# Three of eight expert products split into fp32r passes, in a one-core kernel of two feed-forward layers

## The reference, cut to what matters

```python
x = x + ffn0(cond0(x))      # cond0: a matrix per sequence of rank 30; ffn0: eight experts
x = x + ffn1(cond1(x))      # cond1: layer norms with gathered rows; ffn1: four ternary products

# ffn0, the layer of the change
gate = xf @ Wg.T + bg
w    = softmax(top_k(gate, 2))
h    = einsum('td,ehd->teh', xf, W1) + b1          # eight experts, 256 hidden each
h    = gelu(h)
o    = einsum('teh,eoh->teo', h, W2) + b2          # the second product of every expert
out  = sum over the two chosen experts of w * o
```

## Time and profile before

| | us |
|---|---|
| median of 3 runs | 429.69 (429.18 to 429.79) |
| the profiled execution | 429.37 |
| its span, first to last instruction | 427.5 |
| TensorE busy | 412.8 (97%) |
| VectorE busy | 313.6 (73%) |
| ScalarE busy | 292.1 (68%) |
| GpSimd busy | 115.8 (27%) |

### The profile page before, as it was taken

The page is one execution under the profiler, slowest core; times in us unless marked ns, Lnnn a source line. Parts: engine busy times, 40 slices in busy tenths (PEclk is TensorE's granted clock), DMA queues, the critical chain, the costliest instruction groups (busy, mean ns, idle before and its releaser), DMA issues.

```text
span 427.5 us, 5760 instructions
## 1 busy us (share of the span) xinstructions
PE 412.8 (97%) x1812; PEld 269.5 (63%) x1812; DVE 313.6 (73%) x656; ACT 292.1 (68%) x518; POOL 115.8 (27%) x122
## 2 busy tenths in 40 slices
PE   7999899999999999999999999999999999898996
PEld 4755455445566765776567655676577657677774
DVE  5889998978987578648775848678873798666653
ACT  5588877967856864868656783886578475757654
POOL 0138102642624700363162000457034031110000
PEclk9989999999999999999999999999999999999999
DMA  7978646554453350434330250347402210000000
GB/s 263 374 305 229 161 120 182 132 166 117 116 130 114 90 149 20 105 80 131 114 111 20 75 147 2 88 80 193 129 0 66 74 57 2 0 0 25 2 25 27
DMA packets 30360, 45.07 MB, mean 105 GB/s; under 512 B 3733, under 2 KB 22650, under 8 KB 29946
## 3 DMA queue, kind: packets, MB, share of 16 engines
q1 hardware_dynamic: 26413, 34.14, 28.6%
q0 software_dynamic: 3584, 10.49, 7.8%
q10 hardware_dynamic: 333, 0.07, 0.1%
HBM read 40.68 MB, written 4.03 MB: 105 GB/s over the span
## 4 chain that ended last, share of the span: by engine, by line
PE 85%; DVE 4%; ACT 4%; DMA 3%; issue 2%; SPq 1%; POOL 1%; ACTq 0%; DVEq 0%
PE bank L656 23%; PE bank L758 21%; PE bank L794 7%; PE bank L704 7%; PE bank L648 6%; PE bank L743 5%; PE bank L672 2%; PE bank L711 2%; PE bank L841 2%; DMA t_split<-tsS 2%; PE bank L783 1%; DMA muT<-cond_512T_in 1%; ACT mG L908 1%; PE bank L563 1%; SPq L418 1%
## 5 line engine op out<-in xcount | busy, mean ns | idle before, releaser
L656 PE MATMUL bank<-mG,W 128*128 128x512 f32 x256 | 119.6, 593 | 0.0
L908 ACT ACTIVATE mG<-bank,keepP 128x512 f32<-128x512 f32 x128 | 85.3, 687 | 28.5 <-PE bank L648 19.0
L1467 POOL TENSOR_TENSOR rstd<-ve,mhalf 128x4 f32<-128x4 f32 x24 | 32.8, 1365 | 203.7 <-DVE ve L1208 203.6
L1193 DVE TENSOR_TENSOR mG<-mG,gwbs 128x1024 f32<-128x1024 f32 x64 | 77.2, 1218 | 2.1 <-DMA gwbs<-gate_w 1.8
L656 PEld LDWEIGHTS bank<-mG,W 128*128 128x128 f32 x256 | 47.5, 189 | 38.9 <-issue 35.3
L648 PE MATMUL bank<-ts,A 96*128 96x512 f32 x128 | 62.1, 525 | 2.3 <-ACT mG L908 1.6
L973 ACT ACTIVATE G<-bank,keepP 128x512 f32<-128x512 f32 x48 | 32.2, 692 | 27.8 <-PE bank L758 27.7
L1448 POOL DMA_INDIRECT gp<-pgb_in,ixall x32 | 36.3, 1133 | 25.7 <-issue 9.2
L758 PE MATMUL bank<-hB_h,h2w_h 128*128 128x512 f32 x96 | 39.7, 414 | 0.0
L758 PE MATMUL bank<-hA_h,h1w_h 128*128 128x512 f32 x96 | 38.7, 403 | 0.0
L1451 POOL DMA_INDIRECT gcm<-ctm,ixcm x32 | 35.5, 1110 | 9.8 <-issue 9.4
(11 more groups left out here) (243 smaller groups left out, 782.2 us busy)
## 6 DMA issues: line engine op xcount, KB each, us to landing
gwbs<-gate_w SPq DMA_DIRECT2D x32, 512.0 KB, 5.5
keep<-xT_in SPq DMA_DIRECT2D x8, 256.0 KB, 5.0
outT<-keep SPq DMA_DIRECT2D x8, 256.0 KB, 2.4
t_split<-tsS SPq DMA_DIRECT2D x7, 192.0 KB, 6.0
ts<-t_split SPq DMA_DIRECT2D x7, 192.0 KB, 5.9
hs<-h1T_in SPq DMA_DIRECT2D x1, 1024.0 KB, 7.2
W<-W2T_in SPq DMA_DIRECT2D x1, 1024.0 KB, 9.2
hs<-h2T_in SPq DMA_DIRECT2D x1, 1024.0 KB, 11.2
```

Source lines behind the costliest of these rows:

```text
L656: mm = pe.matmul(OACC[:, :], W2[:, e * HC + c, :], mG[n % NMG][:, c, :], start=False, stop=(e == E - 1 and c == HC - 1))
L908: act.activation(mG[e % NMG][:, c % HC, :], HM[n % 2][:, :], ACT.Gelu, bias=b1c[:, c:c + 1]).then_inc(m_gelu, 1)
L1193: dve.tensor_tensor(mine, mine, gate.unsqueeze(1).broadcast_to([P, HC, TT, P]), ALU.mult).then_inc(m_q, 1)
L1467: step(pool.tensor_tensor(rstd[:, n, :], ve[:, n, :], mhalf[:, :], ALU.pow))
```

## The change

From block 3 on (`SB = 3`), the second products of experts 1, 3 and 5 (`SPLIT`) are made in three fp32r passes instead of one fp32 matmul: for each of the two halves low weights times high values, high weights times high values, high weights times low values. That is 15 of the 64 `O` steps. The parts of the hidden values are made after `q`: ScalarE copies `mG` to `MH` (`mh`), VectorE subtracts (`ml`, into `ML`). There is one `MH` and one `ML`, so the `mh` of an expert waits until the split product before it is done. The weights of these experts are split once, in turn 3 (`wsh`, `wsl`).

The room for `MH`, `ML` and the high weights is that of the second gather buffer. From block 3 on all blocks use buffer 0, and the gathers of block b wait until block b-1 has used it (`last = b`). The expert weights come in three transfers instead of one. Two semaphores were merged into one. The lists of turns 2 to 7 are written anew for all engines.

```diff
+    SPLIT = (1, 3, 5)
+    SB = 3
...
-        W2 = sb("W2", [P, NH, P])
+        W2 = sb("W2", [P, NH - len(SPLIT) * HC, P])
+        whole = ExitStack()
+        W2s = sb("W2s", [P, len(SPLIT) * HC, P], stack=whole)
+        whole.close()
+        W2L = sb("W2_l", [P, len(SPLIT) * HC, P], F32R)
...
+        second = ExitStack()
+        gp[1] = sb("gp1", [P, TT, 2 * P], stack=second)
+        gcm[1] = sb("gcm1", [P, TT, 3 * P], stack=second)
+        second.close()
+        MH = sb("m_h", [P, HC, T], F32R)
+        ML = sb("m_l", [P, HC, T], F32R)
+        W2H = sb("W2_h", [P, len(SPLIT) * HC, P], F32R)
...
+        def side(b):
+
+            return b % 2 if b < SB else 0
...
-            load(W2[:, :, :].rearrange("p n d -> p (n d)"), A["W2T"], ld_w2)
+            by_e = A["W2T"].rearrange("p (e w) -> p e w", e=E)
+            load(W2s[:, :, :].rearrange("p (e c) d -> p e (c d)", c=HC), by_e[:, SPLIT[0]:SPLIT[-1] + 1:2, :], ld_w2)
+            load(W2[:, 0:4 * HC, :].rearrange("p (e c) d -> p e (c d)", c=HC), by_e[:, 0:7:2, :], ld_w2)
+            load(W2[:, 4 * HC:5 * HC, :].rearrange("p c d -> p (c d)"), by_e[:, 7, :], ld_w2)
...
             def O_(b, e):
                 n = b * E + e
+                if b >= SB and e in SPLIT:
+                    i = SPLIT.index(e)
+                    pe.wait_ge(w_lo, len(staged) + 1)
+                    pe.wait_ge(m_lo, split_count(b, e))
+                    for c in range(HC):
+                        wh, wl = W2H[:, i * HC + c, :], W2L[:, i * HC + c, :]
+                        hi, lo = MH[:, c, :], ML[:, c, :]
+                        pe.matmul(OACC[:, :], wl, hi, start=False, stop=False)
+                        pe.matmul(OACC[:, :], wh, hi, start=False, stop=False)
+                        mm = pe.matmul(OACC[:, :], wh, lo, start=False, stop=(e == E - 1 and c == HC - 1))
+                    mm.then_inc(o_mm, 1)
+                    return
...
+            def mh(b, e):
+
+                n, k = b * E + e, split_count(b, e) - 1
+                act.wait_ge(m_q, n + 1)
...
+                    act.wait_ge(o_mm, (SB + (k - 1) // len(SPLIT)) * E + SPLIT[(k - 1) % len(SPLIT)] + 1)
+                act.activation(flat(MH), mG[n % NMG][:, :, :].rearrange("p c n -> p (c n)"), ACT.Copy).then_inc(m_hi, 1)
...
+                act.activation(flat(W2H), flat(W2s), ACT.Copy).then_inc(w_hi, 1)
...
+            def ml(b, e):
+
+                n = b * E + e
+                dve.wait_ge(m_hi, split_count(b, e))
+                dve.tensor_tensor(ML[:, :, :], mG[n % NMG][:, :, :], MH[:, :, :].bitcast(F32), ALU.subtract).then_inc(m_lo, 1)
...
+                dve.tensor_tensor(flat(W2L), flat(W2s), flat(W2H).bitcast(F32), ALU.subtract).then_inc(w_lo, 1)
...
                 if b >= 2:
-                    pool.wait_ge(h_ready, b - 1)
-                    pool.wait_ge(s_ready, b - 1)
-                    pool.wait_ge(t_ready, b - 1)
+                    last = b if b >= SB else b - 1
+                    pool.wait_ge(h_ready, last)
+                    pool.wait_ge(s_ready, last)
+                    pool.wait_ge(t_ready, last)
```

Of the lists, GpSimd's of turn 5 shows how the gathers move against the roots:

```diff
-                (5, "tab0 -rt0 tab1 tab2 =rt2 -rt1 -rt2 tab3 rt0 rt1"),
+                (5, "tab0 tab1 tab2 tab3 rt0 -rt2 rt1"),
```

More of the change, by code:

```diff
@@ L308, in weights_done, with w2_of, split_count @@
             eng.wait_ge(w_lo, max((4, 2, 1, 3)[n] for n in ns))
+        def w2_of(e):
+            t, i = (W2s, SPLIT.index(e)) if e in SPLIT else (W2, [q for q in range(E) if q not in SPLIT].index(e))
+            return t[:, i * HC:(i + 1) * HC, :]
+        def side(b):
+            return b % 2 if b < SB else 0
+        def split_count(b, e):
+            return (b - SB) * len(SPLIT) + SPLIT.index(e) + 1
         def wide(v, n):
@@ L651, in O_ @@
                 n = b * E + e
+                if b >= SB and e in SPLIT:
[10 more added lines that the diff above has]
+                    return
                 pe.wait_ge(m_q, n + 1)
                 if n == 0:
-                    pe.wait_ge(ld_w2, 16)
+                    pe.wait_ge(ld_w2, 16 * 3)
                 for c in range(HC):
-                    mm = pe.matmul(OACC[:, :], W2[:, e * HC + c, :], mG[n % NMG][:, c, :], start=False,
+                    mm = pe.matmul(OACC[:, :], w2_of(e)[:, c, :], mG[n % NMG][:, c, :], start=False,
                                    stop=(e == E - 1 and c == HC - 1))
@@ L860, in wh, with wsh @@
                 act.activation(flat(dst), src, ACT.Copy).then_inc(w_hi, 1)
+            def mh(b, e):
+                n, k = b * E + e, split_count(b, e) - 1
+                act.wait_ge(m_q, n + 1)
+                if k == 0:
+                    for s in (t_ready, s_ready, h_ready):
+                        act.wait_ge(s, 2)
+                else:
+                    act.wait_ge(o_mm, (SB + (k - 1) // len(SPLIT)) * E + SPLIT[(k - 1) % len(SPLIT)] + 1)
+                act.activation(flat(MH), mG[n % NMG][:, :, :].rearrange("p c n -> p (c n)"), ACT.Copy).then_inc(m_hi, 1)
+            def wsh():
+                act.wait_ge(o_mm, (SB - 1) * E + SPLIT[-1] + 1)
+                for s in (t_ready, s_ready, h_ready):
+                    act.wait_ge(s, 2)
+                act.activation(flat(W2H), flat(W2s), ACT.Copy).then_inc(w_hi, 1)
             def tch(b):
@@ L1193, in q_, with wsl @@
                 dve.tensor_tensor(mine, mine, gate.unsqueeze(1).broadcast_to([P, HC, TT, P]), ALU.mult).then_inc(m_q, 1)
+            def ml(b, e):
+                n = b * E + e
+                dve.wait_ge(m_hi, split_count(b, e))
+                dve.tensor_tensor(ML[:, :, :], mG[n % NMG][:, :, :], MH[:, :, :].bitcast(F32), ALU.subtract).then_inc(m_lo, 1)
+            def wsl():
+                dve.wait_ge(w_hi, len(staged) + 1)
+                dve.wait_ge(o_mm, (SB - 1) * E + SPLIT[-1] + 1)
+                dve.tensor_tensor(flat(W2L), flat(W2s), flat(W2H).bitcast(F32), ALU.subtract).then_inc(w_lo, 1)
             def x1_(b):
@@ L1222, in hg @@
                     dve.wait_ge(tr_mm[2], b)
-                pw = gp[b % 2]
+                pw = gp[side(b)]
                 step(dve.tensor_tensor(hh[:, :, :], xh[:, :, :], pw[:, :, 0:P], ALU.mult))
@@ L1233, in t_ @@
                     dve.wait_ge(tr_mm[0], b)
-                dve.tensor_tensor(tt[:, :, :], xh[:, :, :], gcm[b % 2][:, :, P:2 * P], ALU.mult).then_inc(t_ready, 1)
+                dve.tensor_tensor(tt[:, :, :], xh[:, :, :], gcm[side(b)][:, :, P:2 * P], ALU.mult).then_inc(t_ready, 1)
             def s_(b):
@@ L1382, in _ @@
                      "flr": partial(fl_tail, TAIL["r"]), "flp": partial(fl_tail, TAIL["p"]),
-                     "for": partial(fo_tail, TAIL["r"]), "fop": partial(fo_tail, TAIL["p"]), "al": lambda i, n: al(n), "am": lambda i: s_m(),
+                     "for": partial(fo_tail, TAIL["r"]), "fop": partial(fo_tail, TAIL["p"]), "ml": ml, "wsl": lambda i: wsl(), "al": lambda i, n: al(n), "am": lambda i: s_m(),
                      "wl": lambda i, n: wl(n), "lm": lambda i: low_sum(), "tcl": lambda i, b: tcl(b), "la": lambda i: low_any(),
@@ L1447, in tables @@
                 j = b * TT + t
-                pool.indirect_dma_start(out=gp[b % 2][:, t, :], out_offset=None, in_=A["pgb"],
+                pool.indirect_dma_start(out=gp[side(b)][:, t, :], out_offset=None, in_=A["pgb"],
                                         in_offset=bass.IndirectOffsetOnAxis(ap=ixall[:, 0, j:j + 1].bitcast(U32), axis=0))\
                     .then_inc(gat[b % 2], 16)
-                pool.indirect_dma_start(out=gcm[b % 2][:, t, :], out_offset=None, in_=CT,
+                pool.indirect_dma_start(out=gcm[side(b)][:, t, :], out_offset=None, in_=CT,
                                         in_offset=bass.IndirectOffsetOnAxis(ap=ixcm[:, j:j + 1].bitcast(U32), axis=0))\
```

28 lines of the change are left out of this document (11 added, 17 removed), and 89 rows, old and new, of the table ORDER.

## The result

| | before | after |
|---|---|---|
| median, us | 429.54 (428.18 to 431.37, 9 runs) | 425.73 (424.32 to 430.11, 9 runs) |
| ratio after / before, 95% interval | | 0.9924 (0.9898 to 0.995) |
| span of the profiled execution, us | 427.5 | 422.5 |
| from `x` of block 1 to `x` of block 7, us | 265.50 | 261.69 |

The changed kernel is faster by 3.8 us. The forecast was 425.7. The agreement with the median is in part luck. The profiled execution of the changed kernel took 424.33 us, 5.0 less than the profiled one before and 1.4 less than the median, and only that execution can be taken apart: the sum forecast 3.7 us less and for blocks 2 to 7 got 3.8, while the rest of the 5.0 lies in the setup and the tail.

The account below looks back on a forecast made before the run. The prediction took TensorE's own work in blocks 3 to 7 to bound the kernel. From 429.4 us it took 5.1 for the passes, added 1.4 for stalls and 0 for the rest: 425.7 us, range 423.8 to 429.4.

Parts of the forecast that it names:

- TensorE is the bound: Blocks 3 to 7: TensorE's own work sets the pace, so work taken from it shortens the time.
- The passes, -5.1: Second products of three experts, blocks 3 to 7: six fp32r passes save 0.34 us each, 5.1 us for 15.
- The stalls, +1.4: TensorE over 225 us of blocks 3 to 7: idles 2.2 us instead of 0.8, waiting for ml or gelus behind mh.
- The price: TensorE's idle share by VectorE's load: 0.4% at 70 to 78%, 5% at 91%; 1% chosen at about 82%.
- Cost 0 for the lists, the weight transfers and the gather buffer: Reordered lists, three weight transfers, gathers after the previous block's last read: no cost, gathers with about 3 us to spare.
- The distance of 18 to 20 us for the gathers: Block 5's last read to block 6's first use of gathered rows: 18 to 20 us, against 15.4 needed.
- Rival 4: Gathers in blocks 3 to 7 come late, slowed by VectorE's and GpSimd's shared port: 435.7 us at 2 us a block; chance 0.05.
- The cover on VectorE and ScalarE: Added copies and subtractions, up to 36 us in the open, lie beside TensorE's work; VectorE about 80%, ScalarE 77% busy.
- rival 3: Split products wait for their ml and VectorE and ScalarE take back all the gain; chance 0.10 the same, 0.08 slower.
- rivals 2 and 3: Rival 2: VectorE and ScalarE fill up and take back much of the gain, 426.9 to 428.7 us; chance 0.22.
- The tail, -1.3 to +0.9: From block 7's x to the end: put at 0, between -1.3 and +0.9 us.
- case 1: TensorE stays the bound, stalls grow 0 to 2.2 us: 424.3 to 426.5, with tail 423.8 to 426.7; chance 0.52.

Follow-up runs that it names:

- e2: Changed kernel with all copies, subtractions and waits kept, but the 15 split products made as fp32 matmuls again: 428.73 us, ratio 0.9995 to before.
- e1: Changed kernel without the split: all products fp32, no parts made, new lists, single gather buffer and three weight transfers kept: 428.7 us, ratio 0.9997 to before.
- e8: Changed kernel with all eight experts of blocks 3 to 7 in three passes, parts made once: 417.56 us, ratio 0.9727 to before.
- e12: Changed kernel with block 5's and 6's first gate weights issued ahead of the store, and the hidden values' parts made once: 423.69 us, ratio 0.9883 to before.
- e9: Changed kernel with the first gate weights of blocks 5 and 6 issued a turn earlier, ahead of the store: 424.3 us, ratio 0.9887 to before.
- e5: The changed kernel timed once more without an edit: 426.02 us, ratio 0.9906 to before.
- e6: Changed kernel with the gathers of gp rows started as soon as hg of the block before has read them: 425.61 us, ratio 0.9898 to before.
- e10: Changed kernel with block 5's and 6's first gate weights ahead of the store and the gp gathers early: 424.38 us, ratio 0.9881 to before.
- e7: Changed kernel with each of the 15 subtractions ml made twice on VectorE: 431.65 us, ratio 1.0054 to before.

## Why the prediction was right, and where it was not

**TensorE is the bound: right.** e2 gives the whole gain back when only the passes are taken away, e1 when passes and parts are, and e8, with 40 split products, is 11 us shorter than e1 in blocks 2 to 7.

**The passes, -5.1: right, and right in size within 0.2.** Take e1 and e12, neither of which has a hole: e12 has the 15 split products and 14 of the 15 copies and subtractions left out. Blocks 2 to 7 are 265.08 and 260.18 us, so the passes alone give -4.9, or 0.33 us for each of 15. The forecast had 0.34 from two single distances, and the same place in e1 and e9 gives 0.35. With the parts made (e9, 260.68) it is -4.4. The 0.28 of e8 is no measure of a pass: there the stalls between the steps are in it.

**The stalls, +1.4: right in size, wrong in place for two thirds.** I put it down to `ml` and to gelus behind `mh`. What the parts cost in the profiles is 0.5 us (260.68 - 260.18, e9 against e12). About half of that is at the one product that waits for its `ml`: 0.17 us of wait, and its passes are 0.07 us slower from start to start; the rest is in steps too short to name. The other part is one hole, 1.0 us in the first profile (261.69 - 260.68), because the gate weights of block 5 stand behind a store's landing in SyncE's list. In other executions it was 2.0 to 2.3 us and cost 3.7 to 4.0 with the clock (e5, e6). The step that failed is the one that went through the engines' lists for covers: it took ScalarE's, VectorE's, TensorE's and GpSimd's, and never SyncE's, although the diff rewrote it. The price had been read off from two stretches by VectorE's busy share, and that its sum came out was chance: e2 has the same work on VectorE and no idle TensorE at all, though with a slower TensorE. One reading of the lists was wrong too: in turn 4 not `g12` but `g13` stands behind `mh` of expert 5, so `H15` and not `H14` depends on it; `g12` stands there in turn 5. It changes nothing in the sum, since no row shows such a wait.

**Cost 0 for the lists, the weight transfers and the gather buffer: right within what was measured.** e1's ratio is 0.9997; in the profiles its blocks 2 to 7 are 0.4 us shorter than before. The distance of 18 to 20 us for the gathers was 17.5, against the 15.4 of my sum. Rival 4 took place in none of the profiles. What I had not priced is that the gathers now run beside block 5's gate weights; e10 against e9 shows no cost of it when these are ahead, and without that it stays open.

**The cover on VectorE and ScalarE: right, with less room than the average says.** The wait of rival 3 was there, once and for 0.17 us. With 18.3 us more on VectorE (e7) four products wait, and the gain turns into a loss. So rivals 2 and 3 were real mechanisms, and what kept them small was each product's own margin, which runs from none to 4.3 us, and not the busy share of 80%.

**The tail, -1.3 to +0.9:** from `x` of block 7 to the end 73.76 us after and 74.06 before, -0.3. The setup, which the forecast left alone, was shorter by 0.4 us at `x` of block 0 and 0.9 at block 1; its granted clock from 20 to 40 us was 1.00 in this profile and 0.91 in that of before, and the same kernel had 0.83 in e5, so I don't count this to the change.

**The sum.** For blocks 2 to 7: -0.4 (lists) - 4.9 (passes) + 0.5 (parts) + 1.0 (hole) = -3.8, measured 265.50 to 261.69; forecast were -5.1 + 1.4 = -3.7. The forecast for `x` of block 7 was 349.5, and it came at 348.74, 0.8 earlier, as the setup was 0.9 shorter. In the rivals' list, case 1 with the tail's bounds added at full size is 423.0 to 427.4, wider than the 423.8 to 426.7 given there; the measured time is inside both. Why the median lies 1.4 us above the profiled execution no profile of a median execution shows: a longer hole and a lower clock in the setup, as in e5, would both do it.

**A better version.** e9 is the changed kernel with `gb0` ahead: ratio 0.9887 to before, against 0.9924 and 0.9906 for the changed kernel. The intervals overlap, so that e9 is the faster is shown by its missing hole and by its profiles, not by the times alone. A fourth split expert with parts of its own was not tried.

## What to carry to other kernels

Where the bound engine gets faster, everything that was just early enough for it becomes a candidate, and the transfers come first: go through the list of the engine that issues them as well, and ask of each load what wait stands ahead of it and how long that wait can last. A prefetch belongs ahead of a store whose landing something behind it waits for. And a saving per step can be read rightly from one pair of rows (0.34 us, against 0.33 over 15 steps), while the difference over many steps also holds the stalls that a faster engine meets (0.28 over 40). It takes both to tell the price of a step from that of a wait. Last, a view of waits that names none doesn't say that there is room: list for each step how long its operand had been ready.
